# Second half of a macaron block: three stages merged into one pipeline of ticks, attention products in four tiles

## What is computed

```
def fp4_quant_dequant(x):                     # blocks of 16
    scale = max(max|x| / 6, 1e-12)
    return GRID[searchsorted(MID, |x / scale|)] * sign(x) * scale
ffn(x)  = fp4(silu(fp4(x) @ fp4(Wg).T) * (fp4(x) @ fp4(Wu).T)) @ fp4(Wd).T      # 128 -> 352 -> 128
attn(x) = softmax(q k / 8) v  over 4 positions, 16 heads of 64, for 1024 columns # in 128 -> 3072, out 1024 -> 128
x = x + 0.5 * ffn(layernorm(x));  x = x + attn(layernorm(x));  x = x + 0.5 * ffn(layernorm(x))
```

## Time and profile before

| | |
|---|---|
| median of 3 runs | 1918.62 us (1917.05 to 1921.89) |
| span of the profiled execution, first to last instruction | 1890.0 us |
| instructions | 31524 |
| busy: PE, DVE, ACT, POOL | 86%, 70%, 49%, 34% |
| first feed-forward with its statistics | 1175.9 to 1317.0 us |
| attention's normalisation | 1317.0 to 1345.4 us |
| attention | 1345.4 to 1741.0 us |
| last feed-forward | 1741.0 to 1890.0 us |

### The profile page before, as it was taken

How to read it: one execution, slowest core, us unless ns; L and a number is a source line. 1 busy time by engine, 2 the same in 40 slices (tenths; PEclk the granted TensorE clock), 3 DMA queues, 4 the chain that set the end, 5 groups by cost and what they waited for, 6 DMA issues and landing times. The chain is left out here.

```text
span 1890.0 us, 31524 instructions
## 1 busy us (share of the span) xinstructions
PE 1634.6 (86%) x10370; PEld 1161.7 (61%) x10375; DVE 1319.8 (70%) x2575; ACT 934.2 (49%) x1659; POOL 643.3 (34%) x802
## 2 busy tenths in 40 slices
PE   6999947999999999998799993675799999997576
PEld 5668835555555555554666783354578888886354
DVE  6635558888878788782754666898876666663897
ACT  2434423788888888885343442332244444443332
POOL 0787633111111111111088763232333333333232
PEclk9999978999999999999699997898799999999899
DMA  6123420111111111110513341001000000000000
GB/s 247 37 77 86 134 75 24 34 29 35 28 29 40 29 34 29 29 29 8 199 42 89 90 126 67 0 1 37 10 2 1 0 0 0 0 0 2 6 20 20
DMA packets 50298, 82.35 MB, mean 44 GB/s; under 512 B 11236, under 2 KB 35236, under 8 KB 49380
## 3 DMA queue, kind: packets, MB, share of 16 engines
q1 hardware_dynamic: 41092, 62.09, 11.5%
q0 software_dynamic: 9088, 18.76, 3.1%
HBM read 43.19 MB, written 31.22 MB: 39 GB/s over the span
## 5 line engine op out<-in xcount | busy, mean ns | idle before, releaser
L1928 DVE TENSOR_REDUCE z_parts<-z_pM 128x4 f32<-128x512 f32 x576 | 373.3, 685 | 98.3 <-PE z_pM L1666 94.6
L1843 ACT ACTIVATE z_Pr<-z_pE 128x512 f32<-128x512 f32 x576 | 322.4, 596 | 86.6 <-PE z_pE L1690 83.9
L1690 PE MATMUL z_pE<-z_QM,z_QK 128*128 128x512 f32 x576 | 250.8, 438 | 9.1 <-DMA z_QM<-z_Q 6.8
L2035 POOL TENSOR_SCALAR_AFFINE_SELECT z_Pr<-z_Pr 128x512 f32<-128x512 f32 x128 | 81.4, 636 | 483.8 <-ACT z_Pr L1843 483.8
L1666 PE MATMUL z_pM<-z_KM,z_Q 128*128 128x512 f32 x576 | 234.5, 411 | 1.5 <-DVE z_Q L1918 0.9
L1460 POOL TENSOR_TENSOR a_pm<-a_Pn,k_mask 128x512 f32<-128x512 f32 x128 | 132.2, 1058 | 233.5 <-PE a_pT L1299 153.4
L1690 PEld LDWEIGHTS z_pE<-z_QM,z_QK 128*128 128x128 f32 x576 | 108.0, 188 | 159.6 <-ACT z_Pr L1843 90.7
L493 POOL DMA_INDIRECT slot_results<-m_yq,m_xq x156 | 151.9, 974 | 73.8 <-ACT m_yq L698 41.7
L469 POOL DMA_INDIRECT slot_rows<-m_XN,m_dest x128 | 129.8, 1014 | 95.0 <-DVE m_dest L787 59.6
L1703 PE MATMUL z_pO<-z_Pr,z_V 128*9 128x512 f32 (+3 forms) x1536 | 159.3, 488 | 0.1
L1393 DVE TENSOR_SCALAR a_kz<-a_pk,s_bqk 64x512 f32<-64x512 f32 x128 | 95.9, 749 | 45.0 <-PE a_pk L1279 42.6
(11 more groups left out here) (294 smaller groups left out, 3770.6 us busy)
## 6 DMA issues: line engine op xcount, KB each, us to landing
slot_rows<-in_c_pad SPq DMA_DIRECT2D x2, 5070.0 KB, 23.5
m_xq<-slot_rows SPq DMA_DIRECT2D x38, 260.0 KB, 3.8
z_QM<-z_Q SPq DMA_DIRECT2D x128, 64.0 KB, 2.0
z_KM<-z_QK SPq DMA_DIRECT2D x60, 128.0 KB, 2.4
m_raw<-in_gu SPq DMA_DIRECT2D x2, 2048.0 KB, 8.6
m_XN<-slot_results SPq DMA_DIRECT2D x8, 512.0 KB, 4.3
m_raw<-slot_results SPq DMA_DIRECT2D x8, 512.0 KB, 5.4
slot_results<-m_yq,m_xq POOLq DMA_INDIRECT x156, 2.2
```

The source lines that it names most:

```text
L1690: mm(pE[e % 2][:, :].rearrange("p (h c) -> p h c", h=4), QK[G % RING][:, kt * P:(kt + 1) * P], QM[half][:, :, q * P:(q + 1) * P], start=Tr ...
L1843: a.activation(Pr[j % 4][:, :, q * P:(q + 1) * P], pE[e % 2][:, :].rearrange("p (h c) -> p h c", h=4), ACT.Exp, scale=DH0 ** -0.5).then_in ...
L1928: v.tensor_reduce(parts[:, qt, kb, :], pM[n % 3][:, :].rearrange("p (h k) -> p h k", h=4), AX.X, ALU.max).then_inc(maxed, 1)
L2035: g_.affine_select(blk, blk, [[0, 4], [1, P]], ALU.is_ge, 0.0, base=0, channel_multiplier=-1).then_inc(selected, 1)
```

## The change

The three stages become one function, `tail_stage`, unrolled in Python over 99 ticks. In each tick every engine issues a fixed list of steps. The first feed-forward's pairs go in at the pace of `FIRST`, attention unit i runs in tick i+12, and the second feed-forward's pairs go in at `SECOND`, as soon as their two tiles have the attention's output. Statistics are taken again tile by tile, and the inverse square root is computed on POOL (`inverse_root`, an initial guess from the bits made on DVE, then three Newton steps), in `CHAINS`. Gate and up share one bank (`gup`) of 2x176 columns, so a pair needs four rounds of product, silu and multiplication. One bank `tf` serves turns, down product and output projection; `p4` and `p5` serve queries, keys, turned weights and values in turn.

In the attention, keys are copied whole, scores and weighted values use 64 rows by 64 columns of the array, 16 products each with 64 moving columns, the two row halves writing to different banks. POOL expands the weights once, PE turns four blocks rather than eight, and the copy of the values moves from DVE to ACT in four pieces. The order of heads in the value and output weights (`inner_head`) is changed on the host side of the inputs to fit.

```diff
-    L_QK, L_S, L_TURN, L_V, L_PV, L_OUT = 0, 1, 11, 11, 12, 13
...
-                        for gp in range(QT):
-                            for g in range(2):
-                                o = gp * P + g * 64
-                                last = mm(pS[g * 64:(g + 1) * 64, gp * P:(gp + 1) * P].rearrange("p (a k) -> p a k", a=2),
-                                          qb[par][:, o:o + 64], kz[par][:, :, o:o + 64],
-                                          start=True, stop=True)
-                        last.then_inc(s_ready, 1)
-                    if on(L_PV):
...
-                        for hh in range(8):
-                            h0 = (hh % 2) * 64
-                            last = mm(pA[h0:h0 + 64, (hh // 2) * P:(hh // 2 + 1) * P], vb[par][:, hh * 64:(hh + 1) * 64],
-                                      pt[par][:, hh * P:(hh + 1) * P], start=True, stop=True)
-                        last.then_inc(pv_ready, 1)
...
-                        for gg in range(2):
-                            g.tensor_tensor(pm[rr % 2][:, :, gg, :, :].rearrange("p h t b -> p h t b"),
-                                            src.rearrange("p (h t) -> p h t", t=SEQ1).unsqueeze(3).to_broadcast([P, 8, SEQ1, PER]),
-                                            mask2[:, gg * PER:(gg + 1) * PER].unsqueeze(1).unsqueeze(1).to_broadcast([P, 8, SEQ1, PER]),
-                                            ALU.mult).then_inc(expanded, 1)
...
+def tail_stage(nc, C, name, Wt, out):
...
+    AHEAD = 12
+    FIRST = {p: p if p < 6 else 6 + 2 * (p - 6) for p in range(NP2)}
+    SECOND = {p: 2 * p + 15 for p in range(NP2)}
+    PAIR = {n: (p, 0) for p, n in FIRST.items()} | {n: (p, 1) for p, n in SECOND.items()}
+    NTH = {n: k for k, n in enumerate(sorted(PAIR))}
+    LAST = max(PAIR) + 3
+    TICKS = range(-1, 2 * LAST + 2)
...
+    NORM_AT = {(10 if w == 0 else 8 + 8 * w): w for w in range(NW)}
+    CHAINS = [(-1, 0, QT, True), (0, QT, NT, True)]
+    for T in TICKS:
+        if T in NORM_AT:
+            CHAINS.append((T, QT * NORM_AT[T], QT * NORM_AT[T] + QT, False))
+        i = T - AHEAD
+        if T % 4 == 0 and 16 <= i < NU + 14:
+            CHAINS.append((T, (i - 14) // 2 - 1, (i - 14) // 2 + 1, True))
...
+    L_S, L_TURN, L_PV, L_OUT = 1, 11, 12, 14
+    HIGH_AT, LOW_AT = {1: 0, 3: 1, 4: 2}, {4: (0, 1), 5: (2, 3), 6: (4, 5), 7: (6, 7), 8: (8,), 9: (9,)}
...
+                def scores(j):
+                    pe.wait_ge(q_kept, j + 1)
+                    pe.wait_ge(k_kept, j + 1)
+                    need(pe, masked, j)
+                    for gp in range(QT):
+                        for g in range(2):
+                            o = gp * P + g * 64
+                            for a in range(2):
+                                r = slice(64 * a, 64 * a + 64)
+                                last = mm(pS[g * 64:(g + 1) * 64, a, gp * 64:(gp + 1) * 64], qb[j % 2][r, o:o + 64], kb[j % 2][r, o:o + 64], start=True, stop=True)
+                    last.then_inc(s_ready, 1)
...
+                def weighted(j):
+                    pe.wait_ge(t_kept, j + 1)
+                    pe.wait_ge(v_kept, j + 1)
+                    need(pe, a_kept, j)
+                    for kk in range(2):
+                        for g in range(2):
+                            for k in (2 * kk, 2 * kk + 1):
+                                for a in range(2):
+                                    r, c = slice(64 * a, 64 * a + 64), (a + k) % 2
+                                    last = mm(pA[c * 64:(c + 1) * 64, a, kk * P + g * 64:kk * P + g * 64 + 64],
+                                              vb[j % 2][r, g * 256 + k * 64:g * 256 + k * 64 + 64], pt[j % 2][r, k * P + g * 64:k * P + g * 64 + 64], start=True, stop=True)
+                    last.then_inc(pv_ready, 1)
...
+                for T in TICKS:
+                    n, i, even = T // 2, T - AHEAD, T % 2 == 0
+                    if T == 3:
+                        make_bias()
+                    if even and n - 1 in PAIR:
+                        turn_x(n - 1)
+                    if not even and n - 3 in PAIR:
+                        turn_h(n - 3, 1)
+                    if 0 <= i < NU:
+                        queries(i)
+                        keys(i)
+                    if n - 1 in PAIR:
+                        gate_up(n - 1, T % 2, 0)
+                    if 0 <= i - L_TURN < NU:
+                        turn_weights(i - L_TURN)
+                    if even and L_OUT <= i < L_OUT + NU:
+                        project((i - L_OUT) // 2)
+                    if not even and n - 3 in PAIR:
+                        down(n - 3)
+                    if n - 1 in PAIR:
+                        gate_up(n - 1, T % 2, 1)
+                    if even and n - 3 in PAIR:
+                        turn_h(n - 3, 0)
+                    if T - 1 in NORM_AT:
+                        turn_rows(NORM_AT[T - 1])
+                    if 0 <= i - L_TURN < NU:
+                        values(i - L_TURN)
+                    if 0 <= i - L_S < NU:
+                        scores(i - L_S)
+                    if 0 <= i - L_PV < NU:
+                        weighted(i - L_PV)
...
+                def keep_values(j):
+                    act.wait_ge(v_ready, j + 1)
+                    need(act, pv_ready, j - 1)
+                    for g in range(2):
+                        for a in range(2):
+                            heads = p5[g * 64:(g + 1) * 64, :].rearrange("p (k a d) -> p a k d", k=4, a=2)[:, a, :, :]
+                            last = a_.activation(vb[j % 2][a * 64:(a + 1) * 64, g * 256:(g + 1) * 256].rearrange("p (k d) -> p k d", k=4), heads, ACT.Copy)
+                    last.then_inc(v_kept, 1)
...
+                def aggregate(k):
+                    for t in range(CHAINS[k][1], CHAINS[k][2]):
+                        last = v.bn_aggr(mv[:, 2 * t:2 * t + 2], stats[:, 6 * t:6 * t + 6])
+                    st.done(last)
+                    t = slice(CHAINS[k][1], CHAINS[k][2])
+                    st.done(v.tensor_scalar(var[:, t], mv[:, :].rearrange("p (t c) -> p t c", c=2)[:, t, 1], EPS, None, ALU.add))
+                    v.tensor_scalar(root[:, t].bitcast(U), var[:, t].bitcast(U), 1, 0x7FFFFFFF, ALU.logical_shift_right, ALU.bitwise_xor).then_inc(aggregated, 1)
...
+                for T in TICKS:
+                    n, i, even = T // 2, T - AHEAD, T % 2 == 0
+                    if T == -1:
+                        aggregate(0)
+                    for step in (0, 1, 2) if even else (5,):
+                        quantise(n, step)
+                    if T == 0:
+                        aggregate(1)
+                    if T == 4:
+                        dve.wait_ge(bias_made, 1)
+                        v.tensor_tensor(bo[:, :], bo[:, :], p5[:, 0:D], ALU.add).then_inc(bo_ready, 1)
+                    if 0 <= i < NU:
+                        if i == 0:
+                            dve.wait_ge(small_loaded, 64)
+                        keep_keys(i)
+                    if n - 1 in PAIR:
+                        product(n - 1, T % 2, 0)
+                    quantise(n, 3 if even else 6)
+                    if even and L_OUT <= i < L_OUT + NU:
+                        add_projected((i - L_OUT) // 2)
+                    if not even and n - 3 in PAIR:
+                        add_back(n - 3)
+                    if n - 1 in PAIR:
+                        product(n - 1, T % 2, 1)
+                    if T - 1 in NORM_AT:
+                        centre_rows(NORM_AT[T - 1])
+                        low_rows(NORM_AT[T - 1])
+                    if 0 <= i - L_S < NU:
+                        compact(i - L_S)
+                    if even:
+                        quantise(n, 4)
+                    if i % CH1 == 0 and CH1 <= i <= NU:
+                        subtract_maximum(i // CH1 - 1)
+                    if i % CH1 == 1 and CH1 < i < NU + CH1:
+                        divide_by_sum(i // CH1 - 1)
+                    if T in NORM_AT:
+                        w = NORM_AT[T]
+                        dve.wait_ge(x_updated, NTH[FIRST[2 * w + 1]] + 1)
+                        remeasure(QT * w, QT * (w + 1))
+                        aggregate(chain_of(QT * w, 1))
+                    if T % 4 == 0 and L_OUT + 2 <= i < L_OUT + NU:
+                        t = (i - L_OUT) // 2 - 1
+                        dve.wait_ge(o_added, t + 2)
+                        remeasure(t, t + 2)
+                        aggregate(chain_of(t, 2))
...
+                g_ = nc.gpsimd
+                def inverse_root(k):
+                    T, t0, t1, centred = CHAINS[k]
+                    t, means = slice(t0, t1), mv[:, :].rearrange("p (t c) -> p t c", c=2)
+                    pool.wait_ge(aggregated, k + 1)
+                    st.count(g_.tensor_scalar(var[:, t], var[:, t], -0.5, None, ALU.mult))
+                    st.done(g_.tensor_scalar(root[:, t], root[:, t], ROOT_SCALE, None, ALU.mult))
```

(42 more changed lines are left out.)

889 lines of the change are left out of this document (355 added, 534 removed).

## The result

The kernel after takes 2027.86 us (median of 4 runs, 2025.37 to 2029.81), the kernel before 1918.46 beside it: a ratio of 1.057, 95% interval 1.0553 to 1.0587. The forecast was 1944, in a range of 1862 to 2005. Slower was right, +26 us was not: it is +109.

A forecast was written before the change was run, and what follows sets the result against it. PE's own sum was the floor, 458 us after the change; tick by tick, with PE's waits behind POOL's chains deciding, the parts gave 740 us against 714.1, +26, so 1944 us, range 1862 to 2005.

The forecast's parts named there:

- Smaller products: Attention on PE: a group of 32 score or weighted-value products takes 0.57 us, not 0.92; a unit costs 1.15 less.
- Dense pair of ticks: Ticks 32 to 53, a feed-forward pair every 2 ticks: 15.2 us per 2 ticks without a chain.
- Sparse four: Steady ticks with a feed-forward pair every 4 ticks: 26.3 us per 4 ticks.
- The new wait: PE's turn waits for weights POOL expands behind its 4.6 us inverse-root chain: 7.6 or 11.2 us dense, 6.5 or 10.1 sparse.
- The low clock: After each wait for expanded weights PE runs at 1.2 GHz for some 5 us, costing 1.8 us.
- 4 pairs at 7.5 and 4.5 for the first norm: Start, up to tick 11: four pairs at 7.5 us, 4.5 for first norm and bias, within a sum of 60.
- Ticks 12 to 22 ... 4 of waits: Ticks 12 to 22, taken as DVE-bound: 62 us in all, of which 4 are waits.
- Ticks 76 to 87 ... 69. The last pair 34: End of the pipeline: 69 us for ticks 76 to 87, without more queries, then 34 for the last pair.
- Outside the span: The 28.6 us between the profiled span, 1890.0, and the runs' median, 1918.6, are not in the sum and stay.
- the waits hidden: Rival: the waits hide because something else is late in those ticks anyway; 1809 us, chance 0.14.
- the row tiles, at the old pace and in single file: Rival: row tiles do not overlap; 0.92 us a group gives 1982 us, chance 0.12; 1.75 gives 2071, chance 0.05.
- short POOL steps: Rival: a dependent POOL step costs 0.15 us, not 0.29, so a chain is 2.3; 1898 us, chance 0.25.

The follow-up runs named there:

- expand_first: Kernel after with POOL's expansion of the weights moved ahead of the inverse roots: 1930.66 us, 1.0051 of before.
- chain_long: Kernel after with six Newton rounds instead of three in each inverse root: 2118.68 us.
- warm_full: Kernel after with 72 idle identity turns on PE per chain ahead, in front of its wait for expanded weights: 2036.09 us.
- norm_early: expand_first with the attention norm's statistics and inverse root two ticks earlier for all windows but the first: 1895.99 us, 1.0037 of before.
- end_half_passes: Kernel after with the last four passes of every quantisation from tick 76 over half the blocks: 1984.87 us, before 1889.34 beside it.
- warm_edges: Kernel after with idle identity turns on PE in the first ticks (up to 12) and the last (from 77): 2035.54 us.
- scores_twice: Kernel after with every group of 32 score products issued twice: 2059.53 us.
- spread_rows_first: norm_early with mid-stage chains behind POOL's scaling, second feed-forwards four ticks later, rows centred ahead of the last quantisation pass: 1897.02 us, 0.9842 of before.
- one_table: expand_first with attention rows a tick later, a pair's chain before the norm's, and Tanh in place of Silu: 1942.16 us.

## Why the prediction was off, step by step

*Smaller products*: right. A group takes 0.47 to 0.52 us, taken 0.57; the 0.12 in it for entering and leaving the mode had no row, and of it 0.05 is left. *Dense pair of ticks* 15.2: measured 8.5+6.5 = 15.0. *Sparse four* 26.3 is near too: ticks 59 to 64 without their chain tick are 5.8, 7.5, 7.0, 5.8, 7.5. *The new wait*: right in place, number and mechanism (expand_first), and in length (chain_long). The chain of 16 takes 4.6 us where DVE lets it, in after at the start:

```profile
1205.84 0.23 POOL L1358 TENSOR_SCALAR f_var<-f_var 128x4 f32<-128x4 f32 x1 [19.24 <-DVE f_root L1194]
...
1210.18 0.23 POOL L1369 TENSOR_SCALAR f_shift<-f_sq 128x4 f32<-128x4 f32 x1
```

In the dense ticks two of the steps are held up by 0.85 us each, so 6.2 (tick 37, above). The ticks with a wait are longer than summed by about that much: ticks 37, 45 and 53 last 17.0 on average and ticks 33, 41 and 49 last 23.3, so 10.5 and 16.8 over the 6.5 of an odd tick without a wait, where the forecast, with 1.8 for the clock, had 9.4 and 15.2. The steady ticks gave back 0.2 a pair. *The low clock*, 1.8 a wait: right in the dense ticks (warm_full).

The step that failed is the sum's treatment of both ends as if they flowed. Three terms of it were mis-sized:

- "4 pairs at 7.5 and 4.5 for the first norm": 7.5 is a pair's sum of DVE work. A pair took 10.0 to 11.4 (the first passes over 960 columns start at 1232.2, 1242.6, 1253.9 and 1263.9), since in the fixed order a pass stands behind a product that stands behind a gate on PE and a silu on ACT, and POOL's rounding of weights stretches DVE's passes to 2.01 us from 1.16. Up to the norm the four took 36.0 us, not 30. The first norm took 12.8 (1268.2 to 1281.1), with a chain of 5.9 of its own, which the forecast had priced at 4.0 elsewhere and left out here. And 29.2 us passed before the first of the four, not 25.4: the chain for the other 28 tiles takes POOL from 1214.59 to 1220.22, ahead of the first scaling, where the forecast had 2. In all +18.
- "Ticks 12 to 22 ... 4 of waits": tick 17 alone is 16.7 long where its neighbours are 3 to 7: chain, centring, turn and rounding in a row. The forecast counted a chain only where an expansion stands behind it, and in tick 16 none does. With the chain two ticks earlier tick 17 takes 9.9 (norm_early), with a longer one 20.1 (chain_long). +10.
- "Ticks 76 to 87 ... 69. The last pair 34": +38. With little attention left beside it, quantisation no longer overlaps the chain. Timeline of after:

```profile
1979.89 0.48 DVE L83 BATCH_NORM_STATS2 k_stats<-k_X 128x6 f32<-128x128 f32 x2
...
1985.40 0.22 POOL L1369 TENSOR_SCALAR f_shift<-f_sq 128x2 f32<-128x2 f32 x1
1985.66 0.88 ACT L1096 ACTIVATE f_src<-k_X,f_shift,f_rstd 128x128 f32<-128x128 f32 x2 [1.63 <-POOL f_shift L1369]
1986.57 1.15 DVE L1216 TENSOR_REDUCE f_am<-f_src 128x60 f32<-128x960 f32 x1 [2.17 <-ACT f_src L1096]
...
1991.62 1.16 DVE L1231 SCALAR_TENSOR_TENSOR f_y<-f_m,f_y 128x960 f32<-128x960 f32 x1
1992.92 0.62 POOL L1383 TENSOR_TENSOR f_q<-f_y,f_neg 128x256 f32<-128x256 f32 x1 [4.52 <-issue]
...
1993.60 0.69 PE L952 MATMUL f_tf<-k_ident,f_q 128*128 128x128 f32 x2 [9.93 <-POOL f_q L1383]
...
2006.15 0.34 DVE L1240 TENSOR_TENSOR f_src<-f_sg,f_gup 128x176 f32<-128x176 f32 x1 [1.10 <-ACT f_sg L1109]
...
2019.07 0.42 DVE L1246 SCALAR_TENSOR_TENSOR k_X<-f_tf,k_X 128x256 f32<-128x256 f32 x1 [7.63 <-PE f_tf L978]
```

Statistics and chain 5.7, normalisation 0.9, passes 6.2, scaling, turn and copy 1.9, four gates 11.8, a second quantisation, its turns and the down product 13: 39.6 us on one pair, and 4 for the store, 43.6 where the forecast had 34. From tick 76 to the last pair's statistics are 97.2 us where it had 69. The pairs there go round in 30 us each (turns of weights at 1896.5, 1926.55, 1957.02), for which the forecast allows 24.3 (4x4.3, a third of 16, and 1.8). The chain of waits calls DVE's passes here "issue" (4.5 us from 1988.4), because POOL's wait on them has no releaser in the records; end_half_passes shows that they are on the path. chain_long says the same of the chain. The low clock at the two ends, for which the forecast had nothing at the start and 5.4 at the end, is some 9 us of the 56 by the estimate from warm_edges.

*Outside the span*: the 28.6 us were put in the right place by luck. Span and run of before came from executions that differ by 23 us in stages that the change does not touch; their total, 1175.9+28.6 = 1204.5, agrees with the 1203.0+1.9 of after.

Of the rivals, the waits hidden (expand_first) and the row tiles, at the old pace and in single file (scores_twice), are refuted; short POOL steps too, at 0.285 a step.

Why the merged pipeline loses at all, so far as it is argued and not shown: its floor is lower, but three serial loops (start, norms, end) now stand where before a stage's 32 tiles shared one statistics pass, and one queue, POOL's, carries the expansion, the chains and the scaling. With the order changed it wins 28 us of tail (spread_rows_first), where the forecast's case of hidden waits had 110.

## What to carry to other kernels

Put a long chain of small dependent steps behind the last result in its queue that another engine waits for, and give its own user the ticks to wait; halving the chain on a fuller engine gained less than that, and when one wait goes, the next is often in the same queue. Price the fill and the drain of a pipeline as a serial path, each engine's step once in a row, and never by an engine's busy sum. Idle work that is to keep a clock up has to end before the wait does, or it costs more than the clock gives back, as in warm_full and warm_edges. Compare two profiles by the changed part alone when the part ahead can vary by 20 us.

## What the hardware showed

DVE and POOL hold each other up. In after, 20 of the chains' small POOL operations take 0.72 to 1.24 us, not 0.2: each starts within a pass of DVE with two inputs in SBUF (L1229 or L1231) and ends 0.05 to 0.1 us behind it, as above, 1492.55+1.05 against 1492.37+1.15. Of the 29 that start within a DVE operation on a PSUM input (L1252) none takes over 0.24. It goes the other way too. Centred rows in after, duration in ns, least, median, most:

```profile
L1294 DVE TENSOR_SCALAR f_xn<-k_X,f_mv,f_rstd x32: 334/341/1422, 1275.9 to 1796.5; 128x128 f32<-128x128 f32 x32
```

The 1422 ns are those that meet POOL's scaling of 1.39 us. The Trainium skill (GPSIMD Engine Reference, Specifications) says that the two share their SBUF interfaces, with contention where DVE has two SBUF inputs or uses a two-port mode; the traces agree, and show that the one waits for the other's whole operation.

And a table load on ACT takes 1.28 us, twice for each of eight windows, since exponential and silu now alternate; the Trainium skill (ScalarE: Activation LUTs, What ACT_TABLE_LOAD costs) has 1283 ns for it and some 1380 more for draining. The duration agrees; the draining does not show in this trace, where ACT's operation before the load of 1491.10 ends at 1491.08 and the next starts at 1492.39, 0.01 behind it. The merged order brought these loads in unseen by the forecast, and one_table shows them hidden in the dense ticks.
